# Four transformer layers on one core: the row maxima turned over by VectorE instead of TensorE, and a planned TensorE order with a preference for the tiling in use

## The reference

```python
def _softmax(x, axis=-1):
    return jax.nn.softmax(x, axis=axis)      # exp(s - max over keys) / sum
...
def _attn(q, k, v, mask):
    scale = 1.0 / np.sqrt(HD)
    s = jnp.einsum('bqhd,bkhd->bhqk', q, k) * scale
    s = jnp.where(mask, s, jnp.finfo(s.dtype).min)
    a = jax.nn.softmax(s, axis=-1)
    return jnp.einsum('bhqk,bkhd->bqhd', a, v)
```

## Time and profile before

| | |
|---|---|
| median of three runs | 2992.43 us |
| the profiled execution, its own time | 2985.79 us |
| its span, first to last instruction | 2984.0 us |
| PE busy | 2822.5 us, 95% |
| PE weight loads busy | 2049.1 us, 69% |
| DVE busy | 1846.7 us, 62% |
| ACT busy | 1486.9 us, 50% |
| POOL busy | 288.1 us, 10% |
| mean granted TensorE clock | 0.97 |

### The profile page before, as it was taken

How to read it: one execution, slowest core, us unless ns; L and a number is a source line. 1 busy time by engine, 2 the same in 40 slices (tenths; PEclk the granted TensorE clock), 3 DMA queues, 4 the chain that set the end, 5 groups by cost and what they waited for, 6 DMA issues and landing times.

```text
span 2984.0 us, 58003 instructions
## 1 busy us (share of the span) xinstructions
PE 2822.5 (95%) x21570; PEld 2049.1 (69%) x21570; DVE 1846.7 (62%) x4668; ACT 1486.9 (50%) x2329; POOL 288.1 (10%) x340
## 2 busy tenths in 40 slices
PE   6889999999999899988899999999989999999999
PEld 5556766766777766665676777777657777776777
DVE  2577556666664466675655757576567767767652
ACT  0334645544545455435356454545655565464654
POOL 0000101000001211101111111111000000000000
PEclk9899999999999999988799999999989999999999
DMA  4444324333432466643534343434235333333320
GB/s 134 151 143 152 110 72 143 112 112 102 129 115 82 152 177 188 204 131 98 177 99 128 106 148 108 146 108 149 78 111 176 115 108 123 112 123 118 122 74 18
DMA packets 279147, 369.41 MB, mean 124 GB/s; under 512 B 32458, under 2 KB 158218, under 8 KB 278556
## 3 DMA queue, kind: packets, MB, share of 16 engines
q1 hardware_dynamic: 246620, 318.63, 35.5%
q10 hardware_dynamic: 32256, 47.07, 4.3%
HBM read 224.49 MB, written 110.97 MB: 112 GB/s over the span
## 4 chain that ended last, share of the span: by engine, by line
PE 71%; DVE 14%; DMA 5%; ACT 3%; issue 3%; SPq 1%; POOL 0%; ACTq 0%; DVEq 0%; POOLq 0%
PE gen L1209 11%; PE gen L1067 10%; PE gen L1158 9%; PE gen L1200 8%; PE gen L1032 8%; DVE row_max L1497 7%; PE score L1133 4%; PE score L1109 3%; PE score L1080 3%; PE gen L1169 3%; PE gen L1041 2%; PE score L1095 2%; PE score L1139 2%; DMA parts_scratch<-parts 2%; PE gen L1118 2%
## 5 line engine op out<-in xcount | busy, mean ns | idle before, releaser
L1319 ACT ACTIVATE probs<-score 128x1024 f32<-128x1024 f32 (+1 forms) x576 | 570.2, 1024 | 365.6 <-PE score L1133 221.1
L1497 DVE TENSOR_REDUCE row_max<-score 128x4 f32<-128x1024 f32 (+1 forms) x640 | 650.5, 1048 | 154.9 <-PE score L1095 96.9
L1200 PE MATMUL gen<-xnT,w_w 128*128 128x256 f32 x1536 | 367.9, 386 | 3.0 <-ACT hT L1341 1.8
L1209 PE MATMUL gen<-w_w,hT 128*128 128x256 f32 x1536 | 354.1, 384 | 4.1 <-ACT hT L1341 2.3
L1351 POOL TENSOR_TENSOR rstd<-var_eps,minus_half 128x2 f32<-128x2 f32 x160 | 113.0, 707 | 2317.1 <-DVE var_eps L1394 2316.1
L1209 PEld LDWEIGHTS gen<-w_w,hT 128*128 128x128 f32 x1536 | 284.4, 190 | 53.4 <-issue 12.6
L1200 PEld LDWEIGHTS gen<-xnT,w_w 128*128 128x128 f32 x1536 | 282.2, 191 | 49.7 <-issue 9.6
L1326 ACT COPY oT<-gen 128x512 f32<-128x512 f32 x224 | 131.3, 589 | 251.2 <-PE gen L1158 246.7
L1341 ACT ACTIVATE hT<-gen,b_b 128x256 f32<-128x256 f32 x384 | 160.2, 473 | 150.7 <-PE gen L1200 149.8
L1264 ACT ACTIVATE xnT<-gen,mod_all 128x256 f32<-128x256 f32 x288 | 147.0, 568 | 151.8 <-PE gen L1041 151.6
L1095 PE MATMUL score<-k_self,q_stack 64*128 64x256 f32 x1536 | 191.8, 342 | 28.0 <-DVE row_max L1497 15.4
(11 more groups left out here) (138 smaller groups left out, 4276.8 us busy)
## 6 DMA issues: line engine op xcount, KB each, us to landing
q_stack<-parts_scratch SPq DMA_DIRECT2D x336, 256.0 KB, 3.7
parts_scratch<-parts ACTq DMA_DIRECT2D x160, 256.0 KB, 2.6
parts_scratch<-parts SPq DMA_DIRECT2D x160, 256.0 KB, 2.8
k_self<-parts_scratch SPq DMA_DIRECT2D x144, 256.0 KB, 4.2
q_stack<-zeros_scratch SPq DMA_DIRECT2D x112, 256.0 KB, 3.9
q_stack<-maxT SPq DMA_DIRECT2D x224, 128.0 KB, 2.7
k_cross<-parts_scratch SPq DMA_DIRECT2D x192, 78.0 KB, 2.5
x_scratch<-x SPq DMA_DIRECT2D x48, 256.0 KB, 3.2
```

Source lines behind the costliest of these rows:

```text
L1200: mm = pe.matmul(buf[:, i * S:i * S + S], w["w1"][:, fc, col:col + P], xnT[s][:, fc, :], start=fc == 0, stop=fc == FC - 1)
L1209: mm = pe.matmul(buf[:, 0:D], hT[:, j, c * P:c * P + P], w["w2"][:, j, :], start=j == 0, stop=j == FFC - 1)
L1319: act.activation(probs[st.probs][0:keys, :, :], score[st.fill.buf][0:keys, :, :].rearrange("p a (r q) -> p (a r) q", r=2), ACT.Exp, bias=k ...
L1497: dve.tensor_reduce(dst, src, AX_X, ALU.max).then_inc(max_done[b], 1)
```

## The change

It has two parts. First, the two TensorE transposes and the copy behind them go; `mx` now ends with four DVE transposes (`dve.transpose`, shown as STREAM_TRANSPOSE), each of 32 partitions by 64 elements, that write `maxT` from `max_tok` directly. `max_tok` shrinks from 128 to 32 columns and `maxT` from 128 partitions to 32. The steps `mT` and `mc` are gone, and with them one use of a `gen` buffer for each. Between the last L1512 and the first transpose there is a wait of DVE on itself (`link`). SyncE's DMA waits for the semaphore `max_turned` of `mx` instead of that of `mc`. Its size is the same. Second, the planner's choice: the weight of a job is 9 in place of 8, and on PE a step whose tiling is the one in use gets a preference worth 2.

```diff
-            "mx": 0.36, "mT": 0.22, "mc": 0.33,
+            "mx": 0.92,
...
         for h in range(HALVES):
             mx = add("mx", h, "dve", maxima[h * n:h * n + n])
-            mT = add("mT", h, "pe", [mx])
-            mc = add("mc", h, "dve", [mT], mT)
-            spread = [add("sd", h, "sp", [mc])]
+            spread = [add("sd", h, "sp", [mx])]
...
-                st = min(can, key=lambda st: (8 * st.job - st.rank, 0))
+                st = min(can, key=lambda st: (9 * st.job - st.rank - 2 * (eng == "pe" and TILES.get(st.name, "whole") == self.tiles), 0))
...
-        max_tok = [sb(f"max_tok{i}", [P, TC, P], F32R) for i in range(MAXIMA)]
+        max_tok = [sb(f"max_tok{i}", [P, TC, 4 * PAIRS], F32R) for i in range(MAXIMA)]
...
-        maxT = [sb(f"maxT{i}", [P, S], F32R) for i in range(MAXIMA)]
+        maxT = [sb(f"maxT{i}", [4 * PAIRS, TC, P], F32R) for i in range(MAXIMA)]
...
-                    sp.wait_ge(*moved(of(st, "mT", h)))
+                    sp.wait_ge(max_turned, of(st, "mx", h).nth_all)
...
-                def transpose_maxima(st):
-                    s = st.slot
-                    pe.wait_ge(max_tok_ready, of(st, "mx", st.j).nth_all)
-                    buf, maxima = fill(st), max_tok[of(st, "mx", st.j).got["max"]]
-                    for c in range(TC):
-                        mm = pe.transpose(buf[:, c * P:c * P + P], maxima[:, c, :].bitcast(F32), ident[:, :])
-                    mm.then_inc(gen_full[st.buf], 1)
...
-                    ins.then_inc(max_tok_ready, 1)
-
-                def maxima_moved(st):
-                    s, h = st.slot, st.j
-                    dve.wait_ge(*filled(st.fill))
-                    dve.tensor_copy(maxT[of(st, "mx", h).got["max"]][:, :], gen[st.fill.buf][:, 0:S]).then_inc(gen_moved[st.fill.buf], 1)
+                    link(ins)
+                    for b in range(P // 32):
+                        ins = dve.transpose(maxT[st.got["max"]][:, :, 32 * b:32 * b + 32].bitcast(F32),
+                                            max_tok[st.got["max"]][32 * b:32 * b + 32, :, :].bitcast(F32))
+                    ins.then_inc(max_turned, 1)
```

More of the change, by code:

```diff
@@ L147, in rings_of @@
     takes, gives = (), ()
-    if name in ("xT", "cT", "qkv", "mT", "oX", "atT", "out", "up", "down"):
+    if name in ("xT", "cT", "qkv", "oX", "atT", "out", "up", "down"):
         takes += ("gen",)
-    if name in ("xe", "ce", "ve", "rt", "mc", "dv", "ae", "res", "ge") or name == "lo" and not blk.rope:
+    if name in ("xe", "ce", "ve", "rt", "dv", "ae", "res", "ge") or name == "lo" and not blk.rope:
         gives += ("gen",)
@@ L304, in attention_steps @@
             maxima.append(add("mr", u, "dve", [rows], rows))
-        spread, mc = [], None
+        spread = []
         for h in range(HALVES):
             mx = add("mx", h, "dve", maxima[h * n:h * n + n])
-            mT = add("mT", h, "pe", [mx])
-            mc = add("mc", h, "dve", [mT], mT)
-            spread = [add("sd", h, "sp", [mc])]
+            spread = [add("sd", h, "sp", [mx])]
             for u in range(h * n, h * n + n):
@@ L768, in dit_stack @@
         c_var_ready, c_rstd_ready, chat_ready = (sem(n) for n in ("c_var_ready", "c_rstd_ready", "chat_ready"))
-        max_tok_ready, hi_done, lo_done = (sem(n) for n in ("max_tok_ready", "hi_done", "lo_done"))
+        max_turned, hi_done, lo_done = (sem(n) for n in ("max_turned", "hi_done", "lo_done"))
         high_stored, low_stored, parts_placed = ([slot_sems(f"{n}{way}_") for way in range(3)]
@@ L964, in place_maxima @@
                     s, h, pairs, src = st.slot, st.j, PAIRS // HALVES, maxT[of(st, "mx", st.j).got["max"]]
-                    sp.wait_ge(*moved(of(st, "mT", h)))
+                    sp.wait_ge(max_turned, of(st, "mx", h).nth_all)
                     sp.dma_start(queries_of(st)[0:P:4, h:PAIRS:FC, :].bitcast(F32),
-                                 src[0:4 * PAIRS, :].bitcast(F32).unsqueeze(1).to_broadcast([4 * PAIRS, pairs, S])).then_inc(rows_ready[h][s], 16)
+                                 src[:, :, :].bitcast(F32).rearrange("p c k -> p (c k)").unsqueeze(1).to_broadcast([4 * PAIRS, pairs, S])).then_inc(rows_ready[h][s], 16)
                 def store_x(st):
@@ L1220, in _ @@
                         score_rows(st)
-                    elif st.name == "mT":
-                        transpose_maxima(st)
                     elif st.name == "ST":
@@ L1507, in negate_maximum @@
                     src = row_max[s][:, :, :].rearrange("p c (q two) -> p c two q", two=2)[:, :, :, h * pairs:(h + 1) * pairs]
-                    dst = max_tok[st.got["max"]][:, :, 0:4 * PAIRS].rearrange("p c (two n) -> p c two n", two=2)
+                    dst = max_tok[st.got["max"]][:, :, :].rearrange("p c (two n) -> p c two n", two=2)
                     high, low = (dst[:, :, :, part * PAIRS + h * pairs:part * PAIRS + (h + 1) * pairs] for part in range(2))
@@ L1569, in _ @@
                         negate_maximum(st)
-                    elif st.name == "mc":
-                        maxima_moved(st)
                     elif st.name == "dv":
```

## The result

The changed kernel takes 2974.94 us at the median of 20 runs, the kernel before 2985.26 us at the median of 20: a ratio of 0.9955, with a 95% interval of 0.9939 to 0.9971. It is 10 us faster, where 80 were forecast, and lies above the range's upper end of 2958.

The account below looks back on a forecast made before the run. TensorE, busy for 2822.5 of 2984.0 us, was taken as the bound. Transposes -60, changes of tiling -20, waits -8 and VectorE +8 gave -80 us, so 2910 us, with a range of 2865 to 2958.

Parts of the forecast that it names:

- The order: Planned order of all engines' steps under the new weights: nothing on or off, with 25 us to either side.
- TensorE's work: TensorE's stream: 224 transpose steps gone, 60 us off; 206 fewer changes of tiling at 0.095 us, 20 us off.
- What VectorE gets: VectorE's mx: four transposes for one copy, 56 us more work; at 14% of the chain 8 us on, bounds 6 and 19.
- VectorE takes the lead: Rival at the mr steps behind each mx: costly transposes make VectorE lead, slower, about 3050 us; chance 0.06.
- Waits: TensorE's waits for its removed transposes and the DMA spreading the maxima shrink: 8 us off, bounds 0 and 20.
- Half of it: Rival around the layer with cross-attention alone: new weights make TensorE wait more, taking back 45 us, 2955 us; chance 0.13.
- The signs in the profile: Profile after: TensorE busy 70 to 90 us less, VectorE 40 to 134 more, TensorE's main-part idle time near 130 us.

Follow-up runs that it names:

- double_mT: Kernel before, same order, with each TensorE transposing step done twice into the same place, 448 more transposes: 1.0090 of before, 27 us slower.
- nx_dve: Kernel before, same order, with four dead VectorE transposes and a wait on itself behind each of the 160 steps that normalise x: 1.0243 of before.
- before_dve: Kernel before, same order, with three dead VectorE transposes behind each mx, 672 in all: 1.0390 of before, 3107.9 us.
- double_turn: Changed kernel, same order, with the four VectorE transposes of each mx done twice, 896 more: 1.0487 of before, 3127.6 us.
- turn_only: Kernel before with the change's first part alone, transposes on VectorE, weight 8 and no tiling preference: 1.0291 of before, 3071.6 us.
- order_only: Kernel before with the change's second part alone, weight 9 and the tiling preference of 2, TensorE's transposes kept: 1.0030 of before.
- weight_only: Changed kernel with the weight of 9 but without the preference for the tiling in use: 1.0053 of before.

## Why the prediction was wrong

The step that failed is the price of VectorE's time: its share of the chain, 14%, was taken as what a microsecond put on it costs. At unchanged orders the runs show 0.52 to 0.78 us in its place. The order, given 25 us to either side, was sized wrong as well, and by more.

- *TensorE's work*, 60 for the transposes and 20 for the changes of tiling: the sum is right, 81 us in the ledger, but partly by luck. double_mT puts the 448 transposes at 49 us, which leaves 32 for the 206 changes, and two pairs of kernels put one change at 0.19 and 0.20 us, not 0.095. One term was too high and the other too low by about as much. What failed besides is that the work was counted at full price: double_mT gives 0.55 for a microsecond of TensorE at the order of before, so that 80 us are worth some 45.
- *What VectorE gets* is the step that failed. Its time in use was 136 us where the prediction took 56, just past its bound of 134: the four transposes stand end to end, as the rule named there had it. The larger error is the price. The prediction multiplied by VectorE's 14% of the chain, and bounded it by the same 14%. Measured with added transposes, it is 0.52 (nx_dve), 0.67 (before_dve) and 0.78 (double_turn): at 0.67, 136 us cost 91 us, not 8, and the bound of 19 was no bound. The rival "VectorE takes the lead" named this mechanism, but asked 2.5 us for each `mx` before it decides; it got 0.61. One of the two stretches in which the prediction saw VectorE lead was also misread: from 1300 to 1350 us VectorE is busy for 36.9 us, but TensorE for 43.9, so VectorE doesn't lead there. And the L1512 that the earlier trace rows call a lone one is the first of a pair, cut off by the end of the window.
- *Waits.* 8 us less were forecast, 47 more were found in the profiled execution, and up to 37 us of clock that stood in no term. 38 of the 47 are "issue" waits, 35 of them before a first pass; those for row maxima and for `xhat` add 12 each, and what went with L1118 is taken off. How much of the 38 is VectorE's lateness and how much the new weights', no run tells: each part alone brings 16.
- *The order*, put at nothing with 25 us to either side, is what turned a loss into a small gain. By the prices above, VectorE's 91 against TensorE's 45, the change should have cost 46 us; turn_only lost 87, the changed kernel gained 13 by its ratio, and six orders of its steps span 119 us. The term was sized by the idle time of one stretch. Which way the order would fall was not to be had from the rows, so that the change came out faster at all is luck as much as anything in the sum. "Half of it" expected the new weights to cost 45: order_only has them at 9 without the transposes, and with the transposes they gave 100.
- *The signs in the profile.* TensorE's busy time fell by 44 us, not 70 to 90, and is 93% of the span, not 95%. The transposes' 0.97 us and VectorE's 136 us more lie just beyond the upper ends that were written, 0.95 and 134; the DMA on `maxT` is issued 1.5 us after the start of `mx` (601.04 to 602.53), not 1.1. The idle time of the main part, forecast near 130 us, is 183, past the 30 us of growth at which the prediction called itself wrong. Both causes that it named for that case show in the waits, the row maxima and a later job's inputs.

A rule of the Trainium skill, page VectorE: DVE Perf Modes, sections Terms and Rules for kernel authors, was weighed in the prediction and put second to the pair of L1512. For these transposes the trace agrees with the page: 4 x 233 ns in 0.97 us. For the pair of L1500 it does not: two of 0.17 us are over in 0.24.

Two things stay open. No run shows whether VectorE's transposes or TensorE's would win if the planner's numbers were searched for both alike; the best order found with the first is 0.9892, with the second, its copy on ACT, 0.9920. And the prices come from time that was added; only replanned kernels had time taken off.

## What to carry to other kernels

An engine's share of the chain that ended last is not the price of a microsecond added to it. Here four engines run fixed orders through two score buffers, and the engine at 62% cost 0.5 to 0.8 for each microsecond added, the one at 95% about 0.55. Adding dead instructions at an unchanged order measures it in one run each. Where a planner writes the order, try several values of its parameters, and its true costs, before judging a change: here one step of a weight moved the time more than the change did.

## What the runs showed of the hardware

- A VectorE transpose of 32 partitions by 64 elements in float32 takes 232 to 240 ns. Four in a row don't overlap, though they are independent (896 of them are busy for 209.0 us), while two of L1500, of 8 elements, are over in 0.24 us where one takes 0.17. The four each read another group of 32 partitions and the two of L1500 the same ones; no run tells whether it is that or the kind of instruction.
- A transpose of 128 by 128 in float32 added to TensorE's stream is 0.11 us more of work (double_mT, 448 of them), where its own duration is 0.30 us. A change of tiling goes with 0.19 to 0.20 us (order_only against before, weight_only against changed).
- Waits of 2 to 3 us were mostly followed by 1.2 GHz. In the changed kernel's trace there are 13 such waits of TensorE behind the prologue; the mean clock of the 4 us behind them is 0.50 to 0.68 for eleven and 1.00 for two (1261 and 1593 us). Such waits cost up to half as much again: from before to before_dve TensorE has 77 us more of idle time and at most 42 us more at the lower clock.
